# Three joint rounds of a two-layer network on one core: each half of the experts' products one place later among the score products

## The reference: what is computed

```python
x = layernorm(x + gated_attention(x))    # groups of 32 tokens, plus a linear part over 512
x = layernorm(x + experts(x))            # 8 experts of 128 x 128, the best 2 by softmax gate
x = layernorm(x + linear_attention(x))   # 16 heads of 8, softmax feature maps, causal sums
x = layernorm(x + product_key_ffn(x))    # 8 heads, 8 of 1024 rows each of down and up
```

## Time and profile before

| what | us |
|---|---|
| runs of the kernel | 543.49, 541.26, 538.53 |
| their median | 541.26 |
| the profiled execution's own time | 539.87 |
| its span in the profile | 538.1 |
| DVE busy | 467.9 (87% of the span) |
| PE busy | 395.5 (73%) |
| ACT busy | 301.9 (56%) |
| POOL busy | 184.9 (34%) |
| mean granted TensorE clock | 0.761 of full speed |

### The profile page before, as it was taken

How to read it: one execution, slowest core, us unless ns; L and a number is a source line. 1 busy time by engine, 2 the same in 40 slices (tenths; PEclk the granted TensorE clock), 3 DMA queues, 4 the chain that set the end, 5 groups by cost and what they waited for, 6 DMA issues and landing times. The chain is left out here.

```text
span 538.1 us, 16083 instructions
## 1 busy us (share of the span) xinstructions
PE 395.5 (73%) x6356; PEld 275.1 (51%) x6356; DVE 467.9 (87%) x2068; ACT 301.9 (56%) x636; POOL 184.9 (34%) x210
## 2 busy tenths in 40 slices
PE   2996679887697779868436874848697969695575
PEld 1652466545564566438333334646355555555575
DVE  5488898789989978897896899999999999999993
ACT  1443455166644845225642669392978787878651
POOL 3453229522393418821451450404031304040001
PEclk9999795789879985985865885666667575858577
DMA  4810000000000000000000000000000000000000
GB/s 94 230 40 0 1 2 1 2 1 0 2 2 1 1 1 2 1 1 0 1 2 1 1 1 4 4 3 12 4 14 2 13 3 13 3 13 2 14 2 21
DMA packets 12474, 6.95 MB, mean 13 GB/s; under 512 B 3183, under 2 KB 11759, under 8 KB 12399
## 3 DMA queue, kind: packets, MB, share of 16 engines
q1 hardware_dynamic: 11366, 5.65, 4.1%
q10 hardware_dynamic: 1032, 0.27, 0.2%
HBM read 4.87 MB, written 1.05 MB: 11 GB/s over the span
## 5 line engine op out<-in xcount | busy, mean ns | idle before, releaser
L1900 ACT ACTIVATE hot_last<-iota_f,lo_last 128x128 f16<-128x128 f32 x240 | 73.5, 392 | 0.3 <-DVE lo_last L2026 0.3
L2220 PE MATMUL psum<-hot_w,hot_lo 64*128 64x8 f16 x2688 | 39.8, 165 | 39.4 <-DVE hot_lo L2050 27.0
L2220 PEld LDWEIGHTS psum<-hot_w,hot_lo 64*128 64x128 f16 x2688 | 37.8, 101 | 56.1 <-DVE hot_lo L2050 30.9
L2050 DVE TENSOR_TENSOR hot_lo<-lo_t,iota_lo 128x4096 f16<-128x4096 f16 x24 | 53.5, 2285 | 0.0
L2164 PE MATMUL psum<-x3t,down_t 128*128 128x512 f32 x64 | 45.2, 829 | 2.3 <-PEq L319 1.2
L1806 POOL TENSOR_TENSOR eq<-eq,side_f 128x1024 f16<-128x1024 f16 x14 | 29.0, 2088 | 48.4 <-DVE eq L2004 48.4
L1348 PE MATMUL psum<-we,x1t 128*128 128x512 f32 x64 | 41.2, 758 | 2.3 <-DVE wexp L894 1.1
L1973 DVE FIND_INDEX8 side_i<-side,keysims 128x8 uint32<-128x32 f32 x256 | 41.6, 187 | 0.0
L1814 POOL TENSOR_TENSOR rstd<-rstd,minus_half 128x2 f32<-128x2 f32 x8 | 5.7, 707 | 103.9 <-DVE rstd L2105 103.9
L1434 PE MATMUL psum<-q_hi,k_t 32*128 32x128 f16 x256 | 21.3, 262 | 19.9 <-DVE masked L971 13.3
L697 POOL TENSOR_TENSOR s_lo<-feat,s_hi 128x512 f16<-128x512 f32 x28 | 31.7, 1155 | 11.2 <-ACT s_hi L487 11.2
(11 more groups left out here) (293 smaller groups left out, 1123.1 us busy)
## 6 DMA issues: line engine op xcount, KB each, us to landing
xall<-in_L_attn_x SPq DMA_DIRECT2D x4, 256.0 KB, 4.3
out<-o SPq DMA_DIRECT2D x8, 128.0 KB, 1.8
we<-in_L_ffn_We SPq DMA_DIRECT2D x1, 512.0 KB, 4.7
downn<-in_L_ffn_down SPq DMA_DIRECT2D x1, 512.0 KB, 6.0
upw<-in_L_ffn_up SPq DMA_DIRECT2D x1, 512.0 KB, 7.1
wh<-in_L_attn_W_h SPq DMA_DIRECT2D x1, 256.0 KB, 3.4
keysn<-in_L_ffn_keys_p SPq DMA_DIRECT2D x1, 256.0 KB, 6.5
wqkv<-in_L_attn_w_qkv ACTq DMA_DIRECT2D x1, 192.0 KB
```

The costliest lines, as they stand in the source:

```text
L1900: ins = nc.scalar.activation(hot_last[:, lane], iota_f[:], ACT.Abs, bias=lo_last[:, lane:lane + 1], scale=-1.0)
L2050: nc.vector.tensor_tensor(hot_lo[:, pairs], bc(lo_t[:, lanes].rearrange("p (j s) -> p j s", s=2).unsqueeze(2), [P, LB // 2, P, 2]), bc(v.i ...
L2220: ins = nc.tensor.matmul(bank[2 + q // 2 * 2 + t][:, c:c + EH], low, hot_w[half, i, lane // 2, :, lane % 2], start=(lane % (2 * LB) == 0 a ...
```

## The change

In PE's order of the three joint rounds, S21 now stands ahead of E00, S30 ahead of E01, and S31 ahead of E10. The two halves of E1 are issued together by one call. The order becomes: logits, S20, N0, S21, E00, S30, E01, S31, E10, E11, N1, N2, E2, N3, E3. Nothing is added or taken away, and no other engine's order is changed.

```diff
                         a_logits(a)
                         b_scores(b, 2, (0,))
                         b_numerators(b, 0)
+                        b_scores(b, 2, (1,))
                         a_experts(a, 0, (0,))
-                        b_scores(b, 2, (1,))
+                        b_scores(b, 3, (0,))
                         a_experts(a, 0, (1,))
-                        b_scores(b, 3, (0,))
-                        a_experts(a, 1, (0,))
                         b_scores(b, 3, (1,))
-                        a_experts(a, 1, (1,))
+                        a_experts(a, 1)
                         b_numerators(b, 1)
                         b_numerators(b, 2)
                         a_experts(a, 2)
```

## The result

The change took 544.28 us (median of 20 runs, 538.41 to 546.52) against 540.75 us for the kernel before (20 runs, 533.05 to 545.35), a ratio of 1.0092 with a 95% interval of 1.0056 to 1.0128: about 5 us. This ratio leaves out as slow every run more than 1.5% above the fastest of its kernel, by the recorded times 9 of the 20 of the kernel before and 1 of the change. The medians of all the runs lie 3.5 us apart and their means 3.0 us (542.48 and 539.46, 2.2 us to either side). So the change is slower, by 3 to 5 us. A second set of 12 runs of the change gave 1.0084 (1.0040 to 1.0128). Both kernels' runs spread over more than 7 us with the clock that TensorE was granted, which is why single profiles have to be compared round by round.

What follows compares the result with a forecast made beforehand. The prediction took the joint rounds to be bound by DVE's last-ending waits, above all for N3 behind N1's string. Terms 1.0 + 1.4 + 1.4 = +3.8 us gave 543.7 or 545.1; forecast 544.5 us, range 540.0 to 549.0.

Steps and rivals of the forecast that it cites:

- E00: First half of tile 0's expert products on TensorE; 1.99 us at half clock.
- E01: Second half of tile 0's expert products on TensorE, moved behind S30 by the change.
- E11: Second half of tile 1's expert products on TensorE, ahead of N1; 0.96 us at full clock.
- Step 1: S21 ahead of E00, each joint round: TensorE waits 1.44, 1.43, 1.44 us for DVE's mask of S20.
- Step 2, round 1: E01 behind S30, E1 whole behind S31: N1 moves by the new wait, ScalarE starts later, +1.0 us.
- Step 2, rounds 2 and 3: Same moves, later rounds: the clock's rise moves back as much as the work, +1.4 us each.
- low end: Rounds 2 and 3 with the clock rising about where it did: N1 later by +0.6 and +0.5 us.
- +2.1 us: Sum over three rounds if a 1.4 us pause costs no clock already granted.
- Rival A: Clock stays at half through rounds 2 and 3's expert block: +9.4 us, 550.7; chance 0.2, including cases between it and forecast.
- Rival B: DVE is the bound, its earlier masks pay for the later N3: +0, 541.3 us; chance 0.15.
- Rival C: Faster through full clock in round 1 before S30 is done: -2.7 us together, 538.6; chance 0.1.
- N1's distance: From N0 in rounds 2 and 3: if no longer than before, the forecast is wrong.

Runs made afterwards that it cites:

- pause alone: Kernel before in its own order, with one added wait: E00 waits until DVE has masked S20; 544.0 us, ratio 1.0131.
- second pair: Further profiles of both kernels, nothing altered: the kernel before again (541.0 us, ratio 1.0045) and the change again (544.12 us, ratio 1.0084).
- last move: Kernel before with only E1 issued in one piece behind S31, no wait in front of S21; 550.28 us, ratio 1.0196.
- filled pause: The change with one more matmul (336 columns, result overwritten) between N0 and S21, in most of the wait; 544.25 us, ratio 1.0079.

## Why the prediction was right, and where its sizes were off

The time lies 0.2 us from the forecast of 544.5. That closeness is partly luck, since the runs of either kernel spread over 7 us or more; a loss of 3 to 5 us stands against a sum of 3.8. The direction and the pause were right. The way from the pause to the loss was right only in part.

**Step 1** held: the pause came in all three rounds, 1.27 us by the bracket, 1.4 by the count from E00's place, and the mask of S21 came 0.12 us behind the weights where it had stood 0.67 off. The pause alone, with nothing moved, gave a loss of the same size or more (1.0131), and all six kernels with this pause have a ratio above 1 (the lowest, 1.0032, with 1 in its interval). So the pause is a cause and not a companion. But its 1.4 us are not simply added to the round: at the same rise the change's rounds are 0.6 us longer by the line above.

**Step 2, round 1 (+1.0 us).** In single profiles the round went from 18.8 to 16.9 us, in the second pair from 15.5 to 18.3. By the means of two it is +0.4. The step set the clock's rise just after 100 us and took that for the round's own; the runs show a rise anywhere from 2.6 to 12.5 us after the mask in the same kernel.

**Step 2, rounds 2 and 3 (+1.4 us each)** is the mis-sized term. By the means of two profiles they are +3.3 and +1.9 us. I had moved the clock's rise back by as much as the work; in these two rounds it moved back by 5.6 us on the mean (from 3.6 to 9.1 us after the mask), and by 3.8 us over all six rounds. The low end (+0.6 and +0.5, rise where it was) is about what the order costs at the same rise, 0.6 us, but that rise never occurred in the profiles of the change: the earliest was at 6.3 us. Why the rise moves so far stays open.

**The clock and a short pause.** In the last move's profile the pause was 1.38 us, and the granted clock fell from 1.00 to 0.50 within 1.1 us of its end, in all three rounds; so the pause and the lost clock each count. The Trainium skill (TensorE: Matmul & The Clock Gate, "Why this matters for your kernels") has only longer gaps take the clock away, by which the sum would have been the +2.1 us. The trace disagrees, and the measurement decides.

**Rival A** (half clock through the expert block in rounds 2 and 3) was half true: it is what round 2 of the change's profile shows nearly (rise at 11.2 us) and what rounds 2 and 3 of the pause-alone kernel show outright. By the prediction's own sign, a rise behind 158 us in round 2, that round was A's (162.8 us). A's sum of +9.4 us did not come, since rounds 1 and 3 of that profile rose well ahead of N1 and no round of the second rose behind N1. **Rival B** (DVE absorbs it) fell: DVE's waits for PE in these three groups and the masks of S21 went from 10.3 to 15.6 us, and from 6.0 to 15.8 in the second profiles. **Rival C** (faster by an early rise in round 1): the rise did come earlier in round 1 of the first profile, and the round was 1.9 us shorter, but C asked for a rise before S30 was done (93.6 us), and it came at 94.6. The kernel before itself had this round's rise at 12.5 and at 2.6 us, so no gain of the change can be read from it, and the other rounds outweighed it.

**What would show it**: that DVE's wait for N3 would grow by 0.5 us a round held for rounds 2 and 3 (about 0.5 to 1.64) and not for round 1 (1.65 to 1.66). With E1 in one piece in front of N1 the wait for N3 is 1.6 to 1.7 us in every round, whenever the clock rises, and the rest of the lateness shows as the wait for E11. With an expert half before S31 and one behind, it is 0.5 us in rounds with an early rise and 1.6 in rounds such as round 1 of the kernel before (rise at 12.5 us) and rounds 2 and 3 of the pause alone (at 14): so round 1 had its 1.65 us already, from the clock. The sign of N1's distance held: N1 starts 11.5 and 9.5 us after the mask of S20 in rounds 2 and 3 of the change, 7.9 and 8.4 before.

## What to carry to other kernels

Before a piece is moved ahead on an in-order engine, ask what it waits for and what used to fill that time: here an expert half hid the mask of S20, and moving it behind put a pause of 1.4 us into TensorE's work three times, though DVE's visible wait for the piece that moved ahead went away. A pause isn't a price by itself: the rounds grew by 1.9 us on the mean, of which an estimated 0.6 us is the order and 1.3 us goes with a clock that rose later. A wait that a profile blames on a late producer isn't a reason to issue that producer's work earlier when the producer is itself waiting for the consumer. And where the granted clock changes from run to run, compare a stretch over several profiles, with the time of the rise beside it, before reading a difference of 2 us.

## What the runs showed of the hardware that was not expected

- Beside a pause of 1.38 us on PE at 2.4 GHz the clock fell to 1.2 GHz in all three rounds of the last move alone: 1.1 and 1.0 us behind its end in rounds 1 and 3, 0.3 us ahead of its end in round 2.
- With PE shown busy for 11.00 of 11.00 us, the clock stayed at 1.2 GHz throughout (the filled pause, rounds 1 and 2: 11.0 and 11.9 us after the mask).
- The same kernel had the clock rise 12.5 us after a given instruction in one profile and 2.6 us in another, a difference of 3.3 us in the length of that round. Over fifteen rounds in the old order the length went up by about 0.35 us for each us by which the rise came later.
